# A gated delta-rule layer on one core: a quarter of the z projection ahead of the V transposes, and two projections behind the inversion's first transposes

## The reference, cut to what matters

```python
qkvc = silu(conv(x @ W_qkv.T))              # q, k: 16 heads of 128; v: 32 heads of 128
q, kk = l2norm(repeat(q, 2)), l2norm(repeat(kk, 2))
def step(state, inp):                       # over 256 time steps, 4 batches
    state = state * d_t
    delta = (v_t - k_t @ state) * b_t
    state = state + outer(k_t, delta)
    o = q_t @ state
y = o * silu(z);  y = y * rsqrt(mean(y * y) + 1e-6) * norm_w
out = y @ W_out.T                           # z = x @ W_z.T
```

## Time and profile before

| what | us |
|---|---|
| median of three runs (lowest, highest) | 1980.0 (1975.21, 1981.11) |
| the profiled execution's own time | 1971.39 |
| its span, first to last instruction | 1969.4 |
| layer 1's heads 1 to 14 (733.02 to 1873.94) | 1140.92 |
| one head of these | 79.15 to 83.20 |
| PE busy in the span | 1749.0 (89%) |
| DVE, ACT, POOL busy | 1519.3, 1226.4, 636.4 |
| mean granted TensorE clock | 0.971 |

### The profile page before, as it was taken

One profiled execution on the slowest core, in us unless ns is written; L12 is line 12 of the kernel. 1 busy time (PEld: TensorE's weight loads), 2 busy tenths in 40 slices (PEclk: granted clock), 3 DMA queues, 4 the chain that ended last, 5 costly groups with the idle time before them and its releaser, 6 DMA issues.

```text
span 1969.4 us, 35372 instructions
## 1 busy us (share of the span) xinstructions
PE 1749.0 (89%) x12824; PEld 1303.0 (66%) x12824; DVE 1519.3 (77%) x2421; ACT 1226.4 (62%) x2155; POOL 636.4 (32%) x442
## 2 busy tenths in 40 slices
PE   7899999999899778889888889888988888988976
PEld 5667676767657566667766667666776666756665
DVE  8788888888674787887777878778777787877853
ACT  3253534444355567777677877768767786777862
POOL 2212222231230535336053261432605326144140
PEclk9999999999999899999999999999999999999988
DMA  3011110101032001101101011010110101101000
GB/s 131 32 62 38 54 61 31 61 31 62 3 99 65 17 16 39 33 23 33 56 23 33 23 34 55 23 34 23 33 55 23 33 23 34 55 23 33 7 1 22
DMA packets 51465, 75.66 MB, mean 38 GB/s; under 512 B 3392, under 2 KB 41792, under 8 KB 51184
## 3 DMA queue, kind: packets, MB, share of 16 engines
q1 hardware_dynamic: 51312, 73.55, 11.7%
HBM read 72.29 MB, written 1.25 MB: 37 GB/s over the span
## 4 chain that ended last, share of the span: by engine, by line
PE 39%; DVE 12%; ACT 10%; issue 9%; POOL 2%; ACTq 0%; DVEq 0%; POOLq 0%
PE bank L897 6%; PE bank L731 6%; PE bank L852 5%; PE bank L742 4%; DVE d_sil L1311 4%; PE bank L790 2%; DVE d_Rb L1377 2%; PE bank L800 2%; PE bank L764 2%; POOL d_dec L1629 2%; DVE d_W L1385 2%; PE bank L873 1%; PE bank L875 1%; PE bank L874 1%; ACT d_TT L1149 1%
## 5 line engine op out<-in xcount | busy, mean ns | idle before, releaser
L1311 DVE SCALAR_TENSOR_TENSOR d_sil<-d_pre,d_w,d_sil 128x1024 f32<-128x1024 f32 x192 | 298.1, 1553 | 5.9 <-ACT d_pre L1081 5.6
L1635 POOL TENSOR_TENSOR d_Rb<-d_V,d_ones 128x512 bf16<-128x512 f32 x32 | 48.0, 1511 | 711.0 <-ACT d_V L1110 711.0
L1363 DVE CAST_PREDICATED d_X<-tables_sb,bank 128x512 bf16<-128x512 int32 x192 | 134.3, 700 | 147.6 <-PE bank L790 146.9
L731 PE MATMUL bank<-xnT,d_w 128*128 128x512 f32 x480 | 244.1, 644 | 0.8
L189 PE MATMUL bank<-xnT,a_w 128*128 128x512 f32 x512 | 237.0, 597 | 0.0
L1145 ACT ACTIVATE d_T<-bank 128x512 bf16<-128x512 f32 x160 | 98.5, 616 | 107.4 <-PE bank L800 105.1
L1629 POOL TENSOR_TENSOR d_dec<-d_dec,d_qk 128x384 f32<-128x384 f32 x128 | 133.2, 1064 | 44.2 <-DVE d_N L1344 44.2
L852 PEld LDWEIGHTS bank<-d_W,d_N 128*128 128x128 f32 x1024 | 122.7, 193 | 35.0 <-DVE d_W L1385 22.4
L189 PEld LDWEIGHTS bank<-xnT,a_w 128*128 128x128 f32 x512 | 90.9, 192 | 78.5 <-issue 78.5
L731 PEld LDWEIGHTS bank<-xnT,d_w 128*128 128x128 f32 x480 | 89.2, 202 | 79.3 <-issue 79.3
L489 POOL TENSOR_TENSOR a_hidc<-a_hid,a_comb 128x512 f32<-128x512 f32 x32 | 44.4, 1387 | 295.0 <-DVE a_hid L336 295.0
(11 more groups left out here) (211 smaller groups left out, 4497.9 us busy)
## 6 DMA issues: line engine op xcount, KB each, us to landing
d_dec<-decay_scratch SPq DMA_DIRECT2D x32, 512.0 KB, 5.7
a_w<-w SPq DMA_DIRECT2D x16, 897.0 KB, 4.6
d_w<-w SPq DMA_DIRECT2D x16, 776.0 KB, 4.8
a_comb<-comb_scratch SPq DMA_DIRECT2D x16, 512.0 KB, 5.5
d_dec<-decay_scratch SPq DMA_DIRECT2D x32, 256.0 KB, 6.0
d_wo<-w SPq DMA_DIRECT2D x16, 256.0 KB, 3.0
f_w<-w SPq DMA_DIRECT2D x8, 256.0 KB, 3.7
tables_sb<-tables SPq DMA_DIRECT2D x1, 1056.0 KB, 8.4
```

The source lines that it names most:

```text
L731: last = pe.matmul(psum[bank][:, :], cols(slot, (c * KT + k) * P, P), xnT[:, k, h * HALF:(h + 1) * HALF], start=(k == 0), stop=(k == KT - 1))
L1311: dve.scalar_tensor_tensor(sil[c][:, :, :], pre[c % 2][:, :, tap:tap + S], cols(slot, OC + 4 * c + tap, 1), sil[c][:, :, :], ALU.mult, ALU ...
L1363: dve.copy_predicated(left(Xp[lv][:, v], lv), mask.unsqueeze(1).broadcast_to([P, 8, 64]).rearrange("p n (g w) -> p n g w", w=lv), psum[4 + ...
```

## The change

TensorE's program alone is changed. In each body `project_z(slot, i, 2)` now stands ahead of `turn_v(i)`. The projections (0, 1) and (1, 0) of the next head no longer stand ahead of `invert` but are handed to it in a list, `early`, and run after both sets of the bf16 transposes and ahead of the first corner. Projection (0, 0) stays where it was. Head 15 has no next head, so its list is empty. No instruction is added or taken away, and the other engines' programs are the same.

```diff
-            def invert(i, fill):
+            def invert(i, fill, early):
...
                     for n in range(8):
                         last = pe.transpose(pb[:, n * P:(n + 1) * P], TT[v][:, n, :], identb[:, :])
                     last.then_inc(s["t1_ready"], 1)
+                for f in early:
+                    f()
                 for li in range(len(LEVELS)):
                     corner(li, 0)
...
                 nxt = after(j, slot, i)
+                project_z(slot, i, 2)
                 turn_v(i)
-                project_z(slot, i, 2)
                 pe.wait_ge(s["kq_done"], i * 2 + 2)
...
+                early = []
                 if nxt:
                     p = lambda c, h: (lambda: project(nxt[1], nxt[2], c, h))
...
                     p(0, 0)()
-                    p(0, 1)()
-                    p(1, 0)()
+                    early = [p(0, 1), p(1, 0)]
...
-                invert(i, fill)
+                invert(i, fill, early)
```

## The result

| | before | after |
|---|---|---|
| median (lowest, highest), us | 1977.61 (1970.98, 1981.11), 4 runs | 2000.34 (1998.05, 2002.4), 4 runs |
| ratio to before | | 1.012, 95% interval 1.0096 to 1.0144 |
| profiled execution: own time, span | 1971.39, 1969.4 | 2001.41, 1999.6 |
| mean granted clock | 0.971 | 0.966 |
| heads 1 to 14 | 1140.92 | 1164.20 |

The change costs 22.7 us on the medians (the median of before stands a little lower here, with one run more), against the 24.6 us that were forecast. The spans of the two profiled executions are 30.2 us apart.

A forecast was written before the change was run, and what follows sets the result against it. TensorE was taken to bound the kernel, with the first corner waiting for ACT's late copy Tm. Heads 1 to 14 (14 x 1.36 = 19.0 us), head 0 (4.5) and head 15 (1.1) gave 24.6 on 1980.0: 2005 us, range 1998 to 2012.

The forecast's parts named there:

- What bounds the corner: Before each head's first corner PE waits for ACT's late copy Tm, 32.3 us over heads 1 to 14.
- Part 1: z ahead of the V transposes: DVE's second gate, then kk, TT and Tm come 1.1 us later in each head.
- the second gate: DVE's second z gate in head 7 was to wait about 1.7 us or more for its tanh.
- Part 2: Two projections behind the bf16 transposes: corner 0.3 us later without Part 1, 1.4 us later with it.
- PE's wait at the transposes: Before the bf16 transposes PE was to wait for DVE some 2.5 us a head, 35 us in all.
- Nothing behind the corner gives it back.: Levels, apply and residual, after the corner in each head, were all to be late by the same amount.
- Head 0, 4.5 us, and head 15, 1.1 us: Head 0's corner 4.5 us later; head 15, with no projections to move, charged 1.1 us for Part 1.
- The clock: the same number of slow stretches: Idle time moves before the transposes; half-clock stretches stay at eight in heads 1 to 14, about 1.7 us each.
- the clock is worse: Rival: a slow stretch before the transposes in nearly each head, 24.6 + 10 = 35, about 2015 us; chance 0.13.
- Busy time, which was to stay alike: The profile page's busy time was to stay alike after the change.
- The page's rule on the clock: By the skill's rule, dense projections before the corner end eight slow stretches, sum 11 us; forecast kept 24.6.

The follow-up runs named there:

- filled changed kernel: The changed kernel with projection (0, 0), the one left ahead of the bf16 transposes, computed twice into the same bank: 0.994 of before, 1967.68 us.
- filled kernel before: The kernel before with projection (0, 0) computed twice, ahead of PE's wait for Tm: 0.9886 of before, 1953.05 us.

## Why the prediction was right, point by point

- **What bounds the corner.** Right: ACT's own queue. Taking 1.06 us out of that queue moved the corner by 1.05 us; putting 1.72 us of PE work in front of it moved it by 0.06.
- **Part 1, 1.1 us.** Right in size (1.07 at kk, 1.06 at the corner) and in place: with the tanhs ahead of the copies of V it is gone but for 0.14 us at kk and 0.25 at the corner. One sign came out otherwise: the second gate waits 0.71 us for its tanh and not 1.7, because the first gate, which the prediction left out, already waits 1.35.
- **Part 2, 0.3 us alone and 1.4 us with part 1.** Right in the rows: 0.2 to 0.3 and 1.4 us at full clock. PE's wait at the transposes was put at 2.5 us a head and 35 in all, and is 2.4 and 33.7; PE comes to it 1.06 us later in the head than before, near the 1.1 that was allowed for the late last products.
- **"Nothing behind the corner gives it back."** Slightly wrong. In heads without a slow stretch, the corner-to-corner time is 80.33 us in the filled changed kernel and 79.20 in the filled kernel before, 1.13 and not 1.4 a head. The waits inside the first levels are shorter (0.47 against 0.70 to 0.78 us for the second d_X), so that some 4 us over the kernel return.
- **Head 0, 4.5 us, and head 15, 1.1 us.** Head 15's corner is 1.06 us later after its first instruction. In head 0 the second transposes start 1.0 us later, as forecast, but the two projections behind them took 5.61 us at half clock, and the corner came 6.9 us later after the head's first instruction. In the filled changed kernel, where those two projections take 3.65 us, it comes 4.5 us later, as forecast.
- **The clock: the same number of slow stretches.** This was the mis-sized term. The wait before the transposes drew one in 13 heads of 14, where the wait before the corner drew one in eight. It fell close to the rival "the clock is worse" in its count. Its price was less than I gave it, 22.27 - 20.80 = 1.5 us a head, as the slow stretch partly covers PE's wait for the second copy into TT. Busy time, which was to stay alike, grew on PE from 1749.0 to 1764.7 us with it.
- **The account.** The two profiled spans differ by 30.2 us: 2.8 before layer 1's head 0, where the code is the same, 6.9 within head 0 up to its corner, 21.4 from there to head 15's corner, and -0.9 behind it. In the 21.4, PE's busy time grew by 11.4 us (1071.68 to 1083.04) for the same instructions, which is the clock, and its idle time by 10.0. At full clock the order costs 14 x 1.13 + 4.5 + 1.1 = 21.4 us over the whole kernel, with the forecast terms for heads 0 and 15. That is 3.2 us less than the forecast of 24.6. Against the medians' 22.7 it leaves 1.3 us for the clock, for which the sum had nothing and which is less than the 11.4 us of busy time that the two profiled executions are apart. These two overstate the clock's part: their mean granted clocks are 0.971 and 0.966, while sixteen executions of the kernel before lie between 0.961 and 0.972, with a median of 0.969, and the four of the changed kernel between 0.966 and 0.970. How much of the median's loss is the clock is not settled to some us, and that the forecast lies within 2 us of the measured loss is in part luck: one term was too large, and the other stood at nothing.
- **The page's rule on the clock.** The prediction weighed the Trainium skill's rule (TensorE: Matmul & The Clock Gate, Part 1) that activity brings the clock back, and kept to the trace. The runs bear out both halves: with projections right before the corner, the slow stretches behind it did end (1.96 us in each of heads 1 to 14), and the idle time, having moved, made new ones in front of it.

## What to carry to other kernels

Before an in-order engine's work is moved into one of its waits, ask whose wait it is: here ACT came late by its own queue, and one reordering there gained 28 us where both moves on PE lost. Work that covers a wait is worth its place only until the next wait; the three projections in front of the transposes were covering DVE, and moving two of them uncovered it. When an operation is put ahead of another on one engine, follow the queue of whoever reads the delayed result: the loss came from a tanh and a gate that had nothing to do with V but stood behind its copies.

## What the runs showed that I had not expected

- **More work, less time.** Computing one projection twice in a wait of 2.42 us took the changed kernel from 2000.34 to 1967.68 us, with heads 1 to 14 at a clock of 1.00 in place of 0.97 and no more busy time (1016.35 against 1016.55 us). In the kernel before the same filling gave 20 us. Why slow stretches at the loop's back edge also became fewer, though nothing was added there, is open.
- **POOL slows DVE.** Two of DVE's multiplications of 128x384 in fp32 took 4.13 us while POOL scaled y (1.90 and 2.21 us for 128x1024 each), against 1.03 us when POOL was held back; DVE's predicated copies, beside POOL's decay products, took 2.94 against 1.37. A reordering on ACT and DVE that was meant only to have operands ready earlier went from 0.9838 to 1.022, and to 0.983 once POOL was told to wait. The Trainium skill (SBUF — State Buffer, Who interferes with whom) says that a DVE instruction with two SBUF inputs contends with a GpSimd instruction that reads SBUF. It also says that the order of issue decides who blocks whom. The trace agrees for the multiplications into N, both of whose inputs are in SBUF: they took 4.13 against 1.03 us, and in each pair POOL's instruction had started first.
- The fastest kernels here, at 0.983 and 0.9838, both keep the old order on TensorE.
